# Second cross attention of a two-layer gated transformer: softmax denominators summed onto every row of a head, reciprocals of 128x512 in four pieces

## What is computed

```python
x = x + jnp.tanh(g_xattn[1]) * _L1_xattn_ref(_layernorm(x, axis=-1), ctx_512, ctx_512, ...)

def _L1_xattn_ref(q, k, v, q_norm_w, k_norm_w, w_out):      # B=4, T=512, 16 heads of 32, 4 key heads
    q, k = _rms_norm(q, q_norm_w), _rms_norm(k, k_norm_w)
    ...                                                      # heads, rotary embedding
    scores = jnp.einsum('bgnqd,bgkd->bgnqk', qg, k) * scale
    scores = jnp.where(causal, scores, -1e30)
    attn = jax.nn.softmax(scores, axis=-1)
    out = jnp.einsum('bgnqk,bgkd->bgnqd', attn, v)
    ...
    return out @ w_out.T
```

## Time and profile before

| | us |
|---|---|
| median of 3 runs | 858.55 (858.49 to 858.88) |
| the profiled execution | 858.79 |
| its span in the profile | 856.9 |
| TensorE busy, whole span | 661.0 |
| VectorE busy, whole span | 653.3 |
| ScalarE busy, whole span | 611.2 |
| GpSimd busy, whole span | 358.2 |
| mean of one reciprocal L1647 (16 of them) | 0.949 |

### The profile page before, as it was taken

How to read it: one execution, slowest core, us unless ns; L and a number is a source line. 1 busy time by engine, 2 the same in 40 slices (tenths; PEclk the granted TensorE clock), 3 DMA queues, 4 the chain that set the end, 5 groups by cost and what they waited for, 6 DMA issues and landing times. The chain is left out here.

```text
span 856.9 us, 13546 instructions
## 1 busy us (share of the span) xinstructions
PE 661.0 (77%) x5101; PEld 357.2 (42%) x5134; DVE 653.3 (76%) x1042; ACT 611.2 (71%) x812; POOL 358.2 (42%) x436
## 2 busy tenths in 40 slices
PE   5863266776758666679989898989999787888886
PEld 2431123332323233445654564456545433444443
DVE  1689999999999998785884499556634438888884
ACT  2787698998977896488875587569927226776775
POOL 0113514345495565273373147311303316555551
PEclk9997589998987998779989998999999899999999
DMA  8900220000000000622231021122200010010011
GB/s 316 367 1 0 97 51 0 1 1 1 1 1 1 0 1 0 210 79 69 80 116 35 2 69 35 47 69 61 89 1 2 1 35 1 26 37 26 25 37 50
DMA packets 21760, 43.71 MB, mean 51 GB/s; under 512 B 3904, under 2 KB 8512, under 8 KB 20800
## 3 DMA queue, kind: packets, MB, share of 16 engines
q1 hardware_dynamic: 21696, 42.85, 14.6%
HBM read 38.61 MB, written 4.19 MB: 50 GB/s over the span
## 5 line engine op out<-in xcount | busy, mean ns | idle before, releaser
L1630 DVE TENSOR_REDUCE c_nmax<-c_s 128x1 f32<-128x384 f32 (+3 forms) x176 | 108.6, 634 | 84.0 <-PE c_s L1848 83.9
L1748 ACT ACTIVATE c_probs<-c_e 128x512 f32<-128x512 f32 (+1 forms) x176 | 94.6, 559 | 59.0 <-PE c_e L1878 57.9
L1560 POOL TENSOR_TENSOR c_psum<-c_probs 128x1536 f32<-128x1536 f32 x16 | 55.9, 3493 | 157.0 <-ACT c_probs L1748 157.0
L1331 PE MATMUL b_y<-w2q,b_q2T 128*128 128x512 bf16 x254 | 73.4, 443 | 57.6 <-ACT b_q2T L1248 28.2
L2184 PE MATMUL d_gu<-gateq,d_xqT 128*128 128x512 bf16 (+1 forms) x382 | 83.4, 362 | 18.5 <-ACT d_xqT L2109 16.1
L1845 PE MATMUL c_s<-c_kT,c_qaT 96*128 96x128 f16 (+3 forms) x256 | 73.9, 321 | 19.4 <-DVE c_nmax L1630 17.8
L1876 PE MATMUL c_e<-c_qaT,c_kT 98*128 98x512 f16 (+3 forms) x256 | 70.0, 307 | 5.1 <-ACT c_qaT L1735 4.6
L1302 PE MATMUL b_up<-shared,b_xqT 128*128 128x512 bf16 x242 | 68.5, 402 | 3.9 <-ACT hidden L1214 2.6
L1331 PEld LDWEIGHTS b_y<-w2q,b_q2T 128*128 128x128 bf16 x256 | 25.9, 109 | 96.8 <-issue 46.0
L2184 PEld LDWEIGHTS d_gu<-gateq,d_xqT 128*128 128x128 bf16 x384 | 34.9, 98 | 53.5 <-ACT d_xqT L2109 23.0
L1848 PE MATMUL c_s<-c_mask,ident_b 128*128 128x128 bf16 x256 | 53.4, 233 | 0.0
(11 more groups left out here) (237 smaller groups left out, 1853.9 us busy)
## 6 DMA issues: line engine op xcount, KB each, us to landing
c_stage<-in_gateT SPq DMA_DIRECT2D x16, 704.0 KB, 4.0
c_stage<-in_downT SPq DMA_DIRECT2D x6, 768.0 KB, 4.6
xs<-in_x SPq DMA_DIRECT2D x4, 1024.0 KB, 17.5
a_w1f<-in_w1T SPq DMA_DIRECT2D x2, 2048.0 KB, 16.1
hidden<-in_w2T SPq DMA_DIRECT2D x2, 2048.0 KB, 21.6
out<-xs SPq DMA_DIRECT2D x16, 256.0 KB, 2.0
a_ctxT<-in_ctxT SPq DMA_DIRECT2D x1, 1024.0 KB, 5.0
b_ln_g<-in_ln_g SPq DMA_DIRECT2D x1, 1024.0 KB, 4.6
```

The source lines that it names most:

```text
L1331: last = nc.tensor.matmul(y_ps[:], q2T[:, n % 2, c, :], w2q[:, c, :], start=(c == 0), stop=(c == IC - 1))
L1560: nc.gpsimd.tensor_tensor(psum[:], region(slot, 0)[:, :, P:], region(slot, 1), ALU.add).then_inc(psum_ready, 1)
L1630: nc.vector.tensor_reduce(nmax[:, G % 2, i, n:n + heads], s_ps[u % 2][:, 0:heads * (i + 1) * P].rearrange("p (n k) -> p n k", n=heads), ax ...
L1748: nc.scalar.activation(probs[:, G % 2, at:at + width], e_ps[fill % 3][:, 0:width], ACT.Exp).then_inc(e_read, 1)
```

## The change

`total` now takes bank y and sums with a block of 32 columns of ones, so that all 32 rows of a head get the sum at once, and each query tile has its own 128 columns of the bank, 128x512 in all. The parts are as wide as their data: 128, 384 (psum whole), 256 and 128 columns. `expand`, `pattern`, `chosen` and `rden` are gone, with the instructions that set them up (four copies on VectorE, five memsets on GpSimd) and the semaphores. `inverse_sums` takes the reciprocal in place in PSUM, one query tile (128x128) in each of units 0 to 3 of a group, behind that unit's maximum. `attended` moves from unit 3 to unit 4.

```diff
-    WEIGHED, TOTALLED, EXPANDED, PROJECTED = LAG + 11, LAG + 17, LAG + 20, LAG + 24
+    WEIGHED, TOTALLED, INVERTED, ATTENDED, PROJECTED = LAG + 11, LAG + 17, LAG + 18, LAG + 22, LAG + 24
...
-            def inverse_sums(G):
+            def inverse_sums(G, i):
                 dve.wait_ge(den_done, G + 1)
-                if G:
-                    dve.wait_ge(expanded, G)
-                nc.vector.reciprocal(rden[:], den_ps[:, 0:P]).then_inc(rden_ready, 1)
+                sums = y_ps[:, i * P:(i + 1) * P]
+                nc.vector.reciprocal(sums, sums).then_inc(inverse_ready, 1)

             def attended(G):
                 dve.wait_ge(av_read, G + 1)
-                dve.wait_ge(expanded, G + 1)
+                dve.wait_ge(inverse_ready, (G + 1) * TILES)
...
-                G, r = group(u - TOTALLED - 1)
-                if r == 0 and 0 <= G < GROUPS:
-                    inverse_sums(G)
-                G, r = group(u - EXPANDED - 1)
+                for i in range(TILES):
+                    G, r = group(u - INVERTED - i)
+                    if r == 0 and 0 <= G < GROUPS:
+                        inverse_sums(G, i)
+                G, r = group(u - ATTENDED)
                 if r == 0 and 0 <= G < GROUPS:
                     attended(G)
...
             def total(G):
-                take("tr", rden_ready, G + 1)
+                take("y", attn_ready, G + 1)
                 pe.wait_ge(psum_ready, G + 1)
                 pe.wait_ge(e_read, exp_of(G, PER - 1))
-                parts = [region(G % 2, 0)[:, :, 0:P]] + [psum[:, :, i * P:(i + 1) * P] for i in range(TILES - 1)]
-                parts = [(i, part) for i, part in enumerate(parts)] + [
-                    (i, region(G % 2, k)[:, :, (i - k) * P:(i - k + 1) * P]) for k in (2, 3) for i in range(k, TILES)]
-                for m, (i, part) in enumerate(parts):
+                parts = [(0, region(G % 2, 0)[:, :, 0:P]), (P, psum[:]), (2 * P, region(G % 2, 2)), (3 * P, region(G % 2, 3))]
+                for m, (at, part) in enumerate(parts):
                     for n in range(GROUP):
-                        last = nc.tensor.matmul(den_ps[n * HD:(n + 1) * HD, 0:P], pattern[:, i, :], part[:, n, :],
+                        last = nc.tensor.matmul(y_ps[n * HD:(n + 1) * HD, at:at + part.shape[2]], ones[:, 0:HD], part[:, n, :],
                                                 start=(m == 0), stop=(m == len(parts) - 1))
                 last.then_inc(den_done, 1)
-
-            def expand(G):
-                take("y", attn_ready, G + 1)
-                pe.wait_ge(rden_ready, G + 1)
-                for i in range(TILES):
-                    last = nc.tensor.matmul(y_ps[:, i * P:(i + 1) * P], chosen[:, i, :], rden[:], start=True, stop=True)
-                last.then_inc(expanded, 1)
```

More of the change, by code:

```diff
@@ L1395, in xattn1 @@
     mask = t("mask", [P, P], bf16)
-    pattern, rden = prep.rest[:, 0:P].rearrange("p (t j) -> p t j", t=TILES), prep.rest[:, P:2 * P]
-    chosen = t("chosen", [P, TILES, P])
     kT = t("kT", [P, 2, KV_HEADS, SEQ], fp16)
@@ L1618, in early_out @@
                 nc.vector.tensor_copy(turned_to(what, b), heads_of(early_ps[k])).then_inc(early_read, 1)
-            def choices():
-                for i in range(TILES):
-                    nc.vector.tensor_copy(chosen[:, i, :].rearrange("p (n d) -> p n d", d=HD),
-                                          ident[:].rearrange("p (n c) -> p n c", c=HD)[:, :, i:i + 1].broadcast_to([P, GROUP, HD])
-                                          ).then_inc(setup, 1)
             def maximum(u):
@@ L1955, in _ @@
                     total(G)
-                G, r = group(u - EXPANDED)
-                if r == 0 and 0 <= G < GROUPS:
-                    expand(G)
                 for i in range(TILES):
```

14 lines of the change are left out of this document (3 added, 11 removed).

## The result

The changed kernel takes **866.7 us** (median of 4 runs), the kernel before 858.52 beside it: ratio 1.0103, 95% interval 1.0084 to 1.0123. Run again, beside other kernels, it was 868.31 us for 858.73, 1.0102 (1.0070 to 1.0135). I had forecast 860.1, with a range of 854.8 to 864.8. The sign that I thought likeliest came out, but the size is more than five times the forecast's 0.18%, and the time lies above the range.

What follows compares the result with a forecast made beforehand. TensorE was taken to set the pace between 395 and 660 us, VectorE to be nearly full during preparation, and one chain to run alone at the end. Terms -1.35 -4.95 +0.35 +1.3 +2.3 +3.9 = +1.55 us gave 860.1, range 854.8 to 864.8.

Steps and rivals of the forecast that it cites:

- The sign that I thought likeliest: Whole kernel: slower by over 0.2%, chance 0.46, against 0.20 for faster and 0.34 for within.
- Sums on TensorE: Each group's sums: fewer, wider matmuls over the same columns take 1.69 us for 1.71, so no change.
- The bank, -4.95 us: First group of a batch: sums in the y bank no longer wait for projection 3's residual; all three waits go.
- The expansion, -1.35 us: Of 16 x 0.95 us TensorE work removed, only the slack before ScalarE's copy in G4, G11 and G12 pays.
- that rival: ScalarE's copies come earlier once TensorE feeds them earlier, so most groups earn the expansion's time: about 854 us, chance 0.18.
- The reciprocal, 0.87 us: VectorE: each reciprocal costs 0.87 us; three more per group make 2.6 us, 42 us in all.
- the estimate of 1.07 us: VectorE reciprocal of 128 columns by the Trainium skill page; would put the sum about 2 us higher.
- Light groups, +0.35 us: G0, G4, G8 to G13: VectorE's idle time absorbs the reciprocals, except a maximum 0.4 us late in G10.
- Preparation stretches, +1.3 and +2.3 us: G1 to G3 and G5 to G7, while batches 2 and 3 are prepared: extra reciprocals exceed VectorE's gaps and delay TensorE.
- The walk: Going through profile rows with gaps in place: TensorE 1.15 us late at 442.46, 2.3 us at 527.7 and after.
- The end, +3.9 us: Last groups: reciprocals and next-phase inputs delay G14's product, G15's sums and the projection; bounds 2.4 and 6.
- The rival "the clock pays more": Groups without slack: the expansion's time becomes TensorE idle time and causes half clock; about 863.8 us, chance 0.25.

Runs made afterwards that it cites:

- the bank alone: Kernel before with only the sums moved from the tr to the y bank, one reciprocal and the expansion kept: 852.47 us, ratio 0.9938.
- the kernels with one reciprocal with and without filler: Changed kernel with only the first of four reciprocals per group: 852.2 us with four idle expansion-sized matmuls into the av bank, 857.76 without.
- the filler: Changed kernel, all four reciprocals, plus four unread matmuls of the expansion's size into the av bank where the expansion stood: 868.68 us, ratio 1.0135.
- the second profile: Second profiled execution of the unmodified changed kernel, from its repeat set of runs: 865.10 us, where the first profiled execution took 866.97.
- moving it: Changed kernel with the next phase's two inputs (constant INPUTS_AT) two units later: 861.4 us, ratio 1.0033; 13 units later: 858.63 us, ratio 1.0002.

## Why the prediction was wrong, step by step

- **Sums on TensorE: right.** From the first sum to the next matmul behind them a set takes 1.66 us (669.48 to 671.14).
- **The bank, -4.95 us: right** to 0.1 us in each of the three groups, and by an experiment of its own.
- **The expansion, -1.35 us: the gain right, the price left out.** Against the bank alone G4 gave 0.7 and G12 0.3, as the slack said; G11 gave nothing for 0.31, and G2, which I had left out, gave 0.4. In G9 ScalarE's copy stayed where it was: from the group's first reciprocal to the matmul behind the copy it is 5.40 us before (583.35 to 588.75) and after (587.94 to 593.34). So ScalarE's chain did not move up, as that rival would have it, and I had seen that the expansion's time would turn into idle time. What failed is pricing that idle time at zero. It costs clock: 1.6 us in G9, and, by the kernels with one reciprocal with and without filler, some 5 us in all. How much it costs beside four reciprocals isn't shown, since there the filler gained nothing.
- **The reciprocal, 0.87 us: right.** Mean 0.946 us, and the instruction behind one starts 0.86 us after it (452.99 to 453.85), in place in PSUM. So the row was right to decide, and not the estimate of 1.07 us.
- **Light groups, +0.35 us: too much.** G10 got 0.1 us longer, the others nothing.
- **Preparation stretches, +1.3 and +2.3 us: the failed step.** They cost 3.4 and 3.7 us in the second profile, 1.9 and 6.3 in the first. The walk put the loss into TensorE's big waits at 442.5 and 527.7, which were to grow by 1 to 2 us, and that sign did not come: the first went from 2.74 to 2.65 and 2.63 us in the two profiles, the second from 2.61 to 2.40 and 2.39. At the first TensorE was 0.1 us late, where the walk had 1.15; at the second 1.5, where it had 2.3. The loss stood behind them, in G3 (in the second profile waits of 1.47 and 2.90 us for row maxima, at 451.73 and 458.15, where the kernel before has none) and in G7. I had walked the rows with the durations that they had before. That is right for idle gaps, but L444's 0.74 us was a matter of its start. I had looked at this effect for the key squares (L339), the clip and L255, where the trace of before already showed it, and not for instructions that had just missed a sum of GpSimd. L444's end and the start of the sum were 1.1 us apart, and two reciprocals are 1.7. So the shape of the term, a sum of work minus gaps, was wrong, not only its size: with two of the same 64 reciprocals standing elsewhere, the first stretch costs -0.8 to +0.1 us in place of +3.4, and the kernel some 4 us less. For the second stretch this is not the whole: freed of the meeting it still costs 3.2 and 3.4 us (two profiles), about 1 us over the forecast, and what makes this 1 us stays open.
- **The end, +3.9 us: right** in mechanism and size. The projection starts 17.1 us behind G14's first reciprocal (16 to 17 forecast, 16.9 by the walk), after 5.7 us of idle TensorE (5.5 forecast), with the sums at half clock; behind its start the rest takes 0.5 us less (176.75 for 177.26), as forecast. I costed this as a fixed property of the change; it is a property of a constant that was set for another load, and moving it gives 6 to 9 us by the ratios, of which the profiles show 3.8 and 6.9 in the end itself.
- **The rival "the clock pays more"** came true in part: its idle times did (1.54 us in G0, 1.80 at 518.42, for its 1.5 and 2.0), and the clock did cost time, but in G9, which it does not name, and its 863.8 lacks the larger loss, that of L444 in G3. I gave it 0.25 and let the range end at 864.8, though its own case and L444's would have added up.

What stays open is the exact share of chance: the clock in G2, G3, G6 and G7 differs between executions of one kernel, by up to 2.6 us in a stretch, and one profile for each kernel can't tell its mean. The stretches of the second profile add up to 6.3 us of loss, while the medians say 8.2 and 9.6; the difference can't be placed. Nor was it shown why G9 kept its full clock in two of the ten profiles without an expansion or filler, behind the same wait as in the others.

## What to carry to other kernels

When work moves to an engine, don't only add its time to the gaps: look at which instructions behind it now start under a long instruction of GpSimd, as L444 did here, and which had just escaped it. Work taken from TensorE gains only where TensorE was the last to arrive; where it wasn't, the idle time can cost clock. And split a change into its parts before judging it: here one small part, the bank, was worth 5 to 6 us, and it was hidden under 14 us of loss from the rest.

## What the runs showed of the hardware

- A reciprocal of 128x128 fp32 from PSUM to the same place in PSUM takes 0.946 us in the mean and four in a row 3.40, so 0.82 each behind the first; the one that wrote to SBUF took 0.949. It isn't stretched by a sum of GpSimd beside it (1.76 us for two at 453.52).
- A 128x512 instruction of VectorE (L444) took 0.74 us or 3.77 by whether it started 1.8 us ahead of, or 0.2 us behind, the start of a sum of GpSimd of 3.44 us; started 0.6 us ahead of the sum but 0.7 us before the end of another GpSimd instruction, it took 1.24, and the sum 3.91. Started under a GpSimd instruction it ended 0.54 to 0.56 us behind that one's end in the three cases shown above (457.08 to 457.62, 457.67 to 458.22, 452.58 to 453.14).
- Behind a wait of 1.71 us in G9 the granted clock fell to half in eight profiles of ten, and cost 1.6 us each time; behind 0.94 us or less it did in none of five, and behind 1.54 us in G0 it did not either. In the kernel with one reciprocal, fillers of 1 us in each of 16 groups gave back some 5 us; in the kernel with four they gave back nothing in sum.
